# Placing order, two pieces of coefficients in flight, and a third expert on TensorE in a fused graph and expert kernel

## The reference, cut to what matters

```
x = x + L0_gnn(layernorm(x), src, dst, weight, bias)        # mean over dst's edges of h[src]
x = x + L0_ffn(layernorm(x), edge_index, W_gat, ..., W1, b1, W2, b2)
        # attention scores -> top 2 of 4 gates g; out = sum_e g[e] * (gelu(x @ W1[e] + b1[e]) @ W2[e] + b2[e])
x = x + L1_gnn(layernorm(x), src, dst, edge_type_32, edge_weight1, bases, w_comp)
        # an edge of type r has the matrix sum_b w_comp[r, b] * bases[b], times its weight
x = x + L1_ffn(layernorm(x), Wr, br, W1, b1, W2, b2, gamma, beta)
```

## Time and profile before

| | us |
|---|---|
| median of 3 runs | 2339.01 (2338.85 to 2343.71) |
| the profiled execution | 2346.39 |
| its span, first to last instruction | 2344.6 |
| PE busy in it | 1755.0 (75%) |
| DVE busy | 1318.3 (56%) |
| ACT busy | 673.0 (29%) |
| POOL busy | 1064.7 (45%) |

### The profile page before, as it was taken

One profiled execution on the slowest core, in us unless ns is written; L12 is line 12 of the kernel. 1 busy time (PEld: TensorE's weight loads), 2 busy tenths in 40 slices (PEclk: granted clock), 3 DMA queues, 4 the chain that ended last, 5 costly groups with the idle time before them and its releaser, 6 DMA issues. The chain is left out here.

```text
span 2344.6 us, 36960 instructions
## 1 busy us (share of the span) xinstructions
PE 1755.0 (75%) x8828; PEld 1415.5 (60%) x8829; DVE 1318.3 (56%) x3771; ACT 673.0 (29%) x1497; POOL 1064.7 (45%) x1102
## 2 busy tenths in 40 slices
PE   0666677778775799999977445667776749995996
PEld 0344455555554678777766425666666648883875
DVE  5488866666676621133142577888888861117225
ACT  1010135455551232232211243333343320003221
POOL 0737766565630257777740007777777730000000
PEclk9887677777776679999975577898888879997998
DMA  3313333333322042332350044555555555421001
GB/s 134 106 48 96 103 109 101 102 101 103 108 56 71 1 51 69 89 91 69 97 156 1 28 145 116 153 158 157 159 158 158 158 151 193 144 108 41 1 1 55
DMA packets 166964, 231.35 MB, mean 99 GB/s; under 512 B 35716, under 2 KB 125478, under 8 KB 163558
## 3 DMA queue, kind: packets, MB, share of 16 engines
q0 software_dynamic: 47392, 105.58, 16.7%
q1 hardware_dynamic: 116176, 121.33, 16.6%
q10 hardware_dynamic: 3318, 3.50, 0.4%
HBM read 176.67 MB, written 106.07 MB: 121 GB/s over the span
## 5 line engine op out<-in xcount | busy, mean ns | idle before, releaser
L451 POOL DMA_INDIRECT shared_space<-xn_table,edge_source x391 | 384.9, 984 | 287.6 <-PE part L718 126.0
L451 POOL DMA_INDIRECT edge_rows<-xn_table,edge_source x391 | 381.3, 975 | 291.0 <-POOLq L1160 172.2
L1925 PE MATMUL part<-coef,held 128*128 128x128 f32 x2368 | 353.1, 315 | 173.6 <-ACT held L1915 116.5
L1925 PEld LDWEIGHTS part<-coef,held 128*128 128x128 f32 x2368 | 333.4, 227 | 193.4 <-DVE coef L1935 154.7
L718 PE MATMUL part<-shared_space,hot 128*128 x832 | 320.6, 526 | 112.0 <-DVE shared_space L1043 67.2
L1947 DVE SCALAR_TENSOR_TENSOR window_sums<-window_sums,fine_keep,part 128x256 f32 x592 | 284.3, 480 | 76.3 <-PE part L1925 65.1
L718 PEld LDWEIGHTS part<-shared_space,hot 128*128 128x128 f32 x832 | 195.0, 259 | 168.5 <-issue 141.1
L1915 ACT ACTIVATE held<-edge_rows 128x256 f32 x592 | 197.4, 404 | 315.7 <-POOLq L448 176.0
L1351 POOL DMA_INDIRECT gall<-attention_table,attention_source x256 | 245.3, 958 | 78.0 <-issue 77.7
L1043 DVE TENSOR_TENSOR shared_space<-shared_space,part 128x257 f32 x416 | 174.7, 420 | 69.7 <-PE part L718 25.0
L1935 DVE SCALAR_TENSOR_TENSOR coef<-iota,fine_target,slot_coefs 128x128 f32<-128x128 f32 x592 | 205.3, 348 | 0.0
(11 more groups left out here) (438 smaller groups left out, 2186.5 us busy)
## 6 DMA issues: line engine op xcount, KB each, us to landing
basis_sums<-window_sums SPq DMA_DIRECT2D x75, 1024.0 KB
z<-basis_sums SPq DMA_DIRECT2D x25, 1024.0 KB, 4.8
expert_rows<-ys SPq DMA_DIRECT2D x20, 640.0 KB, 3.5
shared_space<-expert_rows SPq DMA_DIRECT2D x25, 512.0 KB, 5.3
W<-in_L_ffn_W SPq DMA_DIRECT2D x20, 512.0 KB, 4.8
low_rows<-attention_digits SPq DMA_DIRECT2D x32, 256.0 KB, 3.6
xn_table<-shared_space SPq DMA_DIRECT2D x10, 640.0 KB, 3.6
shared_space<-xn_table,edge_source POOLq DMA_INDIRECT x391
```

The source lines that it names most:

```text
L451: pool.indirect_dma_start(rows[:, b % ring, 0:D], None, table, bass.IndirectOffsetOnAxis(ap=esrc[:, b:b + 1].bitcast(U32), axis=0)).then_i ...
L1925: mm = nc.tensor.matmul(part[:, n, c * P:(c + 1) * P], held[n][:, c * P:(c + 1) * P], coef[n][:, :, :].rearrange("p b w -> p (b w)"), star ...
```

## The change

- DVE's parts of a placing step become `carry(b-2)`, `place_of(b-1)`, `tiles_of(b)`, `hots(b+1)`.
- The coefficients: every buffer of a piece exists twice; the transposed one-hots are kept in bf16, and `wcomp` is split once into three bf16 parts that add up to it, so that 12 bf16 matmuls take the place of 4 in f32; the order on PE and DVE lets two pieces be under way.
- PE combines three experts instead of two, DVE one; `mean` and `off` move into another tile's tail to make room.

```diff
--- before.py
+++ after.py
@@ -992,20 +992,20 @@
                     V.tensor_scalar(carried[:, t, :], iotab[:, :], row[k][:, t:t + 1], value[:, ds(b * SORT + t, 1)],
                                     ALU.is_equal, ALU.mult).then_inc(carried_ready, 1)
 
-            def placing(b, k, ii, fill=0, last=False):
-
-                if not last:
-                    hots(b + 1, 1 - k, ii + k)
+            def placing(b, k, ii, fill=0, first=False, last=False):
+
+                if not fill:
+                    if not first:
+                        dve.wait_ge(permuted, b - 2)
+                    carry(b - 2, k)
                 yield
                 if fill != 1:
                     place_of(b - 1, 1 - k)
                 yield
                 tiles_of(b, k).then_inc(tiles_ready, 1)
                 yield
-                if fill != 1:
-                    if fill != 2:
-                        dve.wait_ge(permuted, b - 1)
-                    carry(b - 1, 1 - k)
+                if not last:
+                    hots(b + 1, 1 - k, ii + k)
                 yield
 
             PLACING, WHOLE = 6, float(3 << 22)
@@ -1046,11 +1046,14 @@
                     next(parts, None)
 
             def last_places():
+                dve.wait_ge(permuted, CHUNKS_S - 2)
+                carry(CHUNKS_S - 2, 0)
                 yield
                 yield place_of(CHUNKS_S - 1, 1)
+
+            def last_carried():
                 dve.wait_ge(permuted, CHUNKS_S - 1)
                 carry(CHUNKS_S - 1, 1)
-                yield
 
             for k in range(SETS):
                 places(0, k)
@@ -1077,14 +1080,17 @@
             hots(0, 0, 0)
             for b in range(2):
                 step(PLACED + b, parts=placing(b, b, 0, fill=b + 1))
-            with dve.Fori(1, CHUNKS_S // 2 - 1) as ii:
-                link.enter(ii - 1, 2 * PLACING)
+            for b in range(2, 4):
+                step(PLACED + b, parts=placing(b, b % 2, 1, first=(b == 2)))
+            with dve.Fori(2, CHUNKS_S // 2 - 1) as ii:
+                link.enter(ii - 2, 2 * PLACING)
                 for k in range(2):
                     step(ii * 2 + PLACED + k, parts=placing(ii * 2 + k, k, ii))
-                link.leave(CHUNKS_S // 2 - 2)
+                link.leave(CHUNKS_S // 2 - 3)
             for k in range(2):
                 step(AFTER - 2 + k, parts=placing(CHUNKS_S - 2 + k, k, CHUNKS_S // 2 - 1, last=(k == 1)))
             step(AFTER, parts=last_places())
+            last_carried()
             segments_made = segments()
             step(AFTER + 1, parts=segments_made)
             for _ in segments_made:
@@ -1183,9 +1189,12 @@
         W2 = coefs[:, :, :].rearrange("p k b -> p (k b)")[:, 0:EXPERTS * FC * D].rearrange("p (e f d) -> p e f d", e=EXPERTS, f=FC)
         wcomp, identb = sb("wcomp", [P, QT, BASES]), sb("identb", [P, P], BF16)
         free = W1[0][:, :, :].rearrange("p c f -> p (c f)")
-        relhot = free[:, 0:RELS * RQ // 2].bitcast(BF16).rearrange("p (g r q) -> p g r q", r=RELS, q=QT)
-        relation = free[:, RELS * RQ // 2:RELS * RQ // 2 + RELS * QT // 2].bitcast(BF16).rearrange("p (r q) -> p r q", r=RELS)
-        relhot_t = free[:, RELS * RQ:RELS * RQ + RQ // QT * P].rearrange("p (q e) -> p q e", e=P)
+        relation = free[:, 0:RELS * QT // 2].bitcast(BF16).rearrange("p (r q) -> p r q", r=RELS)
+        relhot = [free[:, RELS * QT // 2:][:, k * RELS * RQ // 2:(k + 1) * RELS * RQ // 2].bitcast(BF16)
+                  .rearrange("p (g r q) -> p g r q", r=RELS, q=QT) for k in range(2)]
+        free = W1[1][:, :, :].rearrange("p c f -> p (c f)")
+        relhot_t = [free.bitcast(BF16)[:, k * RQ // QT * P:(k + 1) * RQ // QT * P].rearrange("p (q e) -> p q e", e=P) for k in range(2)]
+        wparts = sb("wcomp_parts", [P, 3, QT * BASES], BF16)
         relb = sb("slot_relb", [P, KT], BF16)
         b1, b2 = sb("b1", [P, EXPERTS, FC]), sb("b2", [P, EXPERTS, D])
         hid = [sb(f"hid{k}", [P, FC, 2 * HALF]) for k in range(2)]
@@ -1205,6 +1214,7 @@
         begin = sb("first_value", [P, PW])
 
         flags = sb("carry_flags", [P, 2, GW])
+        wrest = flags[:, :, :].rearrange("p n w -> p (n w)")[:, 0:QT * BASES]
         last_top = sb("last_top", [P, GW])
         some_start, carried_to = sb("some_start", [P, 1]), sb("carried_to", [P, 1])
         carry_row = sb("carry_row", [P, 1], I32)
@@ -1224,10 +1234,10 @@
         R0 = 3 * NT * H
         den, score, gate, rank = (rest[:, R0 + n * NT * H:R0 + (n + 1) * NT * H].rearrange("p (t h) -> p t h", h=H) for n in range(4))
         R1 = R0 + 4 * NT * H
-        mean, off = sb("mean3", [P, NT]), sb("off3", [P, NT])
+        mean, off = rest[:, FC * 2 * HALF - 2 * NT:FC * 2 * HALF - NT], rest[:, FC * 2 * HALF - NT:FC * 2 * HALF]
         bg = sb("bg", [P, 3, C16])
         assert H == EXPERTS
-        PE_EXPERTS, AHEAD_Y = 2, 12
+        PE_EXPERTS, AHEAD_Y = 3, 12
         diag = [rest[:, R1 + k * PE_EXPERTS * P:R1 + (k + 1) * PE_EXPERTS * P].rearrange("p (e n) -> p e n", n=P) for k in range(2)]
         TOP = A + 2 * DC * NPAD
         yt = [att.space[:, TOP - (k + 1) * EXPERTS * D:TOP - k * EXPERTS * D].rearrange("p (e d) -> p e d", e=EXPERTS)
@@ -1240,7 +1250,8 @@
         h_ps, y_ps, b_ps = ps[:, 0:2, :], ps[:, 2:4, 0:D], ps[:, 4:6, 0:D]
         lines_ps = ps[0:GW, 7, :].rearrange("p (n q) -> p n q", n=4)
         carry_ps = ps[:, 6, 0:EW]
-        relt_ps, coef_ps = ps[:, 0, :].bitcast(BF16)[:, 0:RQ // QT * P], ps[:, 1, 0:RQ * BASES]
+        relt_ps = [ps[:, k, :].bitcast(BF16)[:, 0:RQ // QT * P] for k in range(2)]
+        coef_ps = [ps[:, 2 + k, 0:RQ * BASES] for k in range(2)]
 
         cleared = sem("cleared2")
         w_in, b_in, w2_in, up_in = sem("w_in"), sem("b_in"), sem("w2_in"), [sem("up_in0"), sem("up_in1")]
@@ -1402,7 +1413,9 @@
             nc.scalar.activation(factor[:, :, :], factor[:, :, :], ACT.Exp).then_inc(carry_replies, 1)
             for i in range(RS):
                 act.wait_ge(relt_ready, i + 1)
-                nc.scalar.activation(relhot_t[:, :, :].rearrange("p q e -> p (q e)"), relt_ps, ACT.Copy).then_inc(relt_copied, 1)
+                if i > 1:
+                    act.wait_ge(coef_ready, i - 1)
+                nc.scalar.activation(relhot_t[i % 2].rearrange("p q e -> p (q e)"), relt_ps[i % 2], ACT.Copy).then_inc(relt_copied, 1)
             act.wait_ge(arg_ready, 1)
             nc.scalar.activation(scale[:, :, :, :], scale[:, :, :, :], ACT.Exp).then_inc(exp_done, 1)
             act.wait_ge(var_ready, 7)
@@ -1525,26 +1538,27 @@
             nc.tensor.matmul(carry_ps[:, 0:GW], run[:, :], ident[0:GW, 0:GW], start=True, stop=True)
             nc.tensor.matmul(carry_ps[:, GW:EW], peak[:, 1:P + 1], ident[0:GW, C16:GW], start=True, stop=True).then_inc(carry_replies, 1)
 
-            pe.wait_ge(bg_in, 16 * (3 + QT))
-
             def turn_relations(i):
                 pe.wait_ge(relhot_ready, i + 1)
+                if i > 1:
+                    pe.wait_ge(relt_copied, i - 1)
                 for q in range(RQ // QT):
-                    mm = nc.tensor.transpose(relt_ps[:, q * P:(q + 1) * P],
-                                             relhot[:, q, :, :].rearrange("p r q -> p (r q)"), identb[:, :])
+                    mm = nc.tensor.transpose(relt_ps[i % 2][:, q * P:(q + 1) * P],
+                                             relhot[i % 2][:, q, :, :].rearrange("p r q -> p (r q)"), identb[:, :])
                 mm.then_inc(relt_ready, 1)
 
             turn_relations(0)
             for i in range(RS):
-                pe.wait_ge(relt_copied, i + 1)
-                if i:
-                    pe.wait_ge(coefs_made, i)
-                for q in range(RQ // QT):
-                    mm = nc.tensor.matmul(coef_ps[:, q * QT * BASES:(q + 1) * QT * BASES], relhot_t[:, q, :],
-                                          wcomp[:, :, :].rearrange("p q b -> p (q b)"), start=True, stop=True)
-                mm.then_inc(coef_ready, 1)
                 if i + 1 < RS:
                     turn_relations(i + 1)
+                pe.wait_ge(relt_copied, i + 1)
+                if i > 1:
+                    pe.wait_ge(coefs_made, i - 1)
+                for q in range(RQ // QT):
+                    for n in range(3):
+                        mm = nc.tensor.matmul(coef_ps[i % 2][:, q * QT * BASES:(q + 1) * QT * BASES], relhot_t[i % 2][:, q, :],
+                                              wparts[:, n, :], start=(n == 0), stop=(n == 2))
+                mm.then_inc(coef_ready, 1)
             for t in range(NT):
                 if t >= 2:
                     pe.wait_ge(x_added, t - 1)
@@ -1624,6 +1638,13 @@
 
             link(V.tensor_tensor(self_arg[:, :, :], asrc, adst, ALU.add))
             leaky(self_arg[:, :, :])
+            dve.wait_ge(bg_in, 16 * (3 + QT))
+            left = wcomp[:, :, :].rearrange("p q b -> p (q b)")
+            for n in range(3):
+                link(V.tensor_copy(wparts[:, n, :], left))
```

(16 more changed lines are left out.)

## The result

The changed kernel takes 2213.06 us (median of 4 runs, 2211.94 to 2213.76) against 2338.93 of the kernel before on the same chip: a ratio of 0.9457, 95% interval 0.9441 to 0.9474. That is 125.9 us less; 148.5 were summed up, and 2190 forecast. Its profiled execution has a span of 2210.2 us and ran 2211.9, so here profile and median agree; between the two profiled spans lie 134.4 us, since the profiled execution of before stood 7 us above its median.

A forecast was written before the change was run, and what follows sets the result against it. Waits bound placing and coefficients, DVE the combination. Gains of 64.5 (placing), 77 (coefficients) and 8 (combination), less 1 for splitting `wcomp`, sum to 148.5 us: forecast 2190 us, range 2158 to 2240.

The forecast's parts named there:

- What the one-hots' move removes: Placing: DVE's whole wait of 3.24 us a step for the one-hots' transfer goes, leaving a floor of 9.6 us.
- What is late next: Placing: the loop through ACT's one column buffer comes next, summed to 10.9 us a step, 9.4 to 12.3 by clock.
- That is the nearest row, so I take 10.7: Placing: step of 12.85 us falls to 10.7, after the last placing step's 10.66; gain 64.5 us, bounds 16 and 97.
- Carrying at nothing: Placing: the last carry waits one step later for the permutation, once, under 2 us; counted as 0.
- Coefficients: Coefficient stage: a piece falls from 3.03 to 0.95 us with two in flight and bf16 matmuls; gain 77 us.
- the far bound of 1.7 us a piece: Coefficients: if each weight load showed its length, a piece takes 1.7 us and the gain is 49 us.
- the cap of 81: Coefficients: POOL's gathers land near 1235 us, so at most 81 us can be gained; below 0.85 a piece buys nothing.
- Combination: Combination: DVE loses one of two operations a tile, PE gains work; gain 8 us, between 11 and -10.
- PE's clock eats the placing: Rival, placing: the freed wait becomes waiting for the permutation, 12.3 us a step; gain 100, 2239 us; chance 0.13.
- Weight loads: Rival, coefficients: each weight load shows its length, gain there 49 us; total 120.5, 2218 us; chance 0.12.
- all floors: Rival, all three parts: every floor is reached, gains 97, 81 and 11 less 1; total 188, 2151 us; chance 0.10.
- slower: Rival: PE falls to 1.2 GHz throughout placing, 15.6 us a step, 83 us lost there; 2356 us; chance 0.03.

The follow-up runs named there:

- act_order_again: The changed kernel with both halves of the comparison ahead of both halves of the columns on ACT; 2165.39 us, ratio 0.9262 to the kernel before.
- hots_last: The kernel before with only the one-hots of the digits moved to a placing step's last part, carrying left one chunk back; 2297.86 us, ratio 0.9828.
- coefs_bf16_one: The kernel before with bf16 parts in the coefficients (12 matmuls a piece) but single buffers; 2288.57 us, ratio 0.9784.
- coefs_f32_two: The kernel before with two coefficient pieces in flight but f32 matmuls kept; 2305.47 us, ratio 0.9855.
- coefs_alone: The kernel before with only the change's coefficients part, bf16 parts and double buffers; ratio 0.9776, in a batch where the kernel before took 3147.2 us.

## Why the prediction was right, and where it was short

- *What the one-hots' move removes.* Right: L977's wait for the transfer fell from 97.0 us to nothing.
- *What is late next.* Right in kind: the loop through ACT's columns, with DVE's new wait on PE (L718) at 79.0 us over the kernel, 54 more than before. That `act_order_again` brings 47.7 us more shows that ACT's columns held the step, though nearly all of it shows as PE's work done faster, at a higher clock.
- *Its price: "That is the nearest row, so I take 10.7".* This is the term that was mis-sized. The loop's own sum stood in the text as 10.9, and the single step of the earlier trace rows was taken in its place; 10.9 would have given 58.5 us, still too much. The window over that step in the trace of before gives a granted clock of 0.84:

```profile
691.40:702.06 10.66, 9.29 (x70) 6.92 (x70) 7.92 (x28) 6.55 (x12) 0.00 (x0) 0.84 0.00 1
```

  It was a turn of the fast kind, like the changed kernel's of 10.8 at 0.84, while every third turn runs at 0.72 and takes 12.2. The stage's mean is 11.4. Against the 12.7 that a step took in the two profiled coefficient kernels, which have the old placing (12.73 and 12.66), that is 39 us in 30 steps; `hots_last` measured 41.0 where 64.5 stood. This one term is 23.5 us, where forecast and median lie 23.1 apart; the errors of the coefficients (3 to 5 too little) and of the combination (3 too much by the traces) nearly cancel, and that is luck.
- *Carrying at nothing.* Right: moving it two back costs nothing that shows, and it gains nothing either.
- *Coefficients.* The price of the 12 matmuls, 0.5 us with the drain at the low level, was right (0.51), and the far bound of 1.7 us a piece is excluded. By the Trainium skill (TensorE: Matmul & The Clock Gate, section LDWEIGHTS (loading the stationary operand)) they would have taken 1.28; 0.34 to issue at 0.50 disagrees. Another section of that page of the Trainium skill, Weight-path perf modes — Fast Weight Load (FWL) and DoubleRow, says that weights of 128 columns that aren't fp32 are read faster, and with that the traces agree: in the changed kernel the loads of the small matmuls are busy for 13.7 us in all for 432, 0.03 each, and in `coefs_bf16_one`, at the clock of 0.50 that the kernel before had, for 14.8 us for 444, as long each, where those of the kernel before have 65.8 for 296 of f32, 0.22 each. The piece came out at 0.79 instead of 0.95, so the term was about 80 to 82 rather than 77. The clock was 0.91 where 0.50 was expected, but that is the smaller part of it: the first three pieces, from 1156.77 to 1159.24 at a mean clock of 0.59, took 0.82 each, and the next eight, at 1.00, 0.75 each. The allowance on top of the loops' own 0.80 and 0.88 was not needed. Behind the loop DVE waits 0.8 us for the gathers to land, so the loop is about as fast as pays, as the cap of 81 had it.
- *Combination.* One of DVE's two operations went, and PE is busy 87% of the stretch, where over 80 was expected. The size, 8, was too high, by 3 as the traces have it. The low start was right in kind: the clock is 0.50 from 1207.7 to 1212 us.
- *The rivals.* "PE's clock eats the placing" (12.3 us a step) points the same way as the miss: one turn in three is that slow. Weight loads, all floors and slower did not come. DVE's floor of 9.6 was not reached by this change, but 9.7 to 9.9 are, once the columns' loop is open.

## What to carry to other kernels

A wait that one engine shows, and a wait of another engine in the same step, may be one loop: follow it round before adding their prices, and cut it where a reordering is cheapest; here four lines on ScalarE were worth as much as the change's placing part, and the two added, for each removed the wait that the other had left. When a step's price is read from a single instance, read the clock granted over that instance too, and compare it with the stage's mean. When a reordering also raises the granted clock, compare busy and idle time per step before calling the gain a removed wait. Of two edits that come together (bf16 parts and a second buffer; moving the one-hots and carrying two back), run each alone: in the first pair each half paid for itself, in the other one half did nothing.

## What the runs showed of the hardware

In `coefs_f32_two` PE was busy for 74.50 of 74.50 us at a granted clock of 0.50 throughout, while in the changed kernel the same stage, busy 26.5 of 28.6 us with 12 bf16 matmuls and 4 transposes a piece, was granted 0.91, and in `coefs_bf16_one`, busy 33.5 of 58.4, 0.50 again. In `coefs_alone` the change's pieces had 0.93. I had expected the opposite of both, the low level for the change and, as the second theory, the high one for the f32 matmuls. What decides it was not tried. In the placing the clock went from 0.77 to 0.80 to 0.89 (0.91 with the carrying one back) as steps got shorter. Whether the clock or the step moved first was not tried either.
